# A recurrence moved two steps ahead on the grid of steps that a whole network shares, with the input products and base chunks dealt out anew

## What is computed

```
# block 0
att  = attention over 8 block sums, one vector per sequence, projected by Wo
n    = layernorm(x + att) * gamma + beta
q()  = block quantisation over groups of 32 values
x1   = x + q(silu(q(n) @ w_gate.T) * (q(n) @ w_up.T)) @ w_down.T      # inner width 2048

# block 1: a GRU over the 256 positions, state [16, 512], then a routed layer
gi   = x1 @ W_ih + b_ih
gh   = h @ W_hh + b_hh
r, z = sigmoid(gi_r + gh_r), sigmoid(gi_z + gh_z)
h    = (1 - z) * tanh(gi_n + r * gh_n) + z * h

hid    = silu(h @ rw1.T + rb1)
logits = hid @ rw2.T + rb2 + gates                # 16 experts, the top 2 are kept
coeff  = softmax of the top 2, zero elsewhere
y      = h @ W.T + bias + ((h @ A.T) * coeff) @ B.T
out    = x1 + y
```

## Time and profile before

| | |
|---|---|
| median of 3 runs | 1708.49 us (1707.1 to 1712.42) |
| the profiled execution: its own time | 1712.84 us |
| its span, first to last instruction | 1711.0 us |
| mean granted TensorE clock | 0.963 of full speed |
| busy: PE, PEld, DVE, ACT, POOL | 91%, 70%, 82%, 38%, 29% |
| granted TensorE clock in 40 slices, tenths of full speed | 9, 8, 6, 6, 6, then 9 in 34 slices and 8 in the last |

### The profile page before, as it was taken

The page is one execution under the profiler, slowest core; times in us unless marked ns, Lnnn a source line. Parts: engine busy times, 40 slices in busy tenths (PEclk is TensorE's granted clock), DMA queues, the critical chain, the costliest instruction groups (busy, mean ns, idle before and its releaser), DMA issues.

```text
span 1711.0 us, 75109 instructions
## 1 busy us (share of the span) xinstructions
PE 1551.7 (91%) x32268; PEld 1198.1 (70%) x32268; DVE 1399.7 (82%) x5571; ACT 644.3 (38%) x1624; POOL 496.8 (29%) x573
## 2 busy tenths in 40 slices
PE   5633689999999999999999999999999999999986
PEld 2321367777777777777777777777777777778874
DVE  7787888888888888888888888888888888887654
ACT  5666243333333333333333333333333333333331
POOL 6774322222222222222222222222222222221000
PEclk9866699999999999999999999999999999999998
DMA  7744211112211111122111112212111212211000
GB/s 245 267 154 135 57 45 43 42 47 49 49 46 49 31 40 49 46 46 50 48 41 49 49 46 49 37 35 47 46 46 49 49 43 46 49 43 37 25 15 20
DMA packets 122444, 101.01 MB, mean 59 GB/s; under 512 B 91904, under 2 KB 92288, under 8 KB 121728
## 3 DMA queue, kind: packets, MB, share of 16 engines
q1 hardware_dynamic: 121824, 96.02, 21.1%
q10 hardware_dynamic: 288, 0.19, 0.0%
HBM read 58.43 MB, written 16.78 MB: 44 GB/s over the span
## 4 chain that ended last, share of the span: by engine, by line
PE 77%; DVE 14%; issue 3%; DMA 2%; POOL 2%; ACT 2%; SPq 0%; DVEq 0%; ACTq 0%; POOLq 0%
PE ps_rn_turn L1311 25%; PE ps_gi L1212 12%; PE ps_z L1311 10%; PE ps_down L1179 6%; PE ps_gate_up L1170 6%; PE ps_gate_up L1160 4%; PE ps_base L1221 4%; PE ps_base L1264 3%; PE ps_route L1221 3%; DVE fe L821 1%; POOL qfT L1028 1%; DVE gi L630 1%; DVE gi L628 1%; DVE hT L808 1%; PE ps_rn_turn L1200 1%
## 5 line engine op out<-in xcount | busy, mean ns | idle before, releaser
L1311 PEld LDWEIGHTS ps_rn_turn<-hT,whh 128*128 128x128 f16 x16320 | 435.0, 96 | 86.0 <-DVE hT L759 72.2
L1311 PE MATMUL ps_rn_turn<-hT,whh 128*128 128x32 f16 x16320 | 449.3, 177 | 46.1 <-DVE hT L759 45.4
L1046 POOL TENSOR_TENSOR qf<-f8c,fe 128x512 bf16<-128x512 bf16 x128 | 134.1, 1047 | 862.1 <-DVE f8c L838 862.1
L583 ACT ACTIVATE r_tanh<-r_pre,scale_half 128x64 f32<-128x64 f32 x256 | 89.0, 348 | 563.5 <-DVE r_pre L779 563.5
L1212 PEld LDWEIGHTS ps_gi<-x1T,wih 128*128 128x128 f16 x4608 | 270.6, 98 | 32.8 <-issue 3.1
L1212 PE MATMUL ps_gi<-x1T,wih 128*128 128x128 f16 x4608 | 289.3, 220 | 1.6 <-ACT gi L574 1.6
L1311 PE MATMUL ps_z<-hT,whh 128*128 128x32 f16 x8160 | 243.3, 177 | 0.0
L1311 PEld LDWEIGHTS ps_z<-hT,whh 128*128 128x128 f16 x8160 | 222.6, 96 | 0.0
L574 ACT ACTIVATE gi<-ps_gi,b_i,scale_x 128x128 f32<-128x128 f32 x384 | 144.4, 456 | 196.7 <-PE ps_gi L1212 196.7
L773 DVE TENSOR_TENSOR r_half<-ps_rn_turn,gi 128x64 f32<-128x64 f32 x256 | 57.2, 224 | 149.9 <-PE ps_rn_turn L1311 146.1
L585 ACT ACTIVATE z_tanh<-z_pre,scale_half 128x64 f32<-128x64 f32 x256 | 89.0, 348 | 157.0 <-DVE z_pre L789 157.0
(11 more groups left out here) (201 smaller groups left out, 2408.5 us busy)
## 6 DMA issues: line engine op xcount, KB each, us to landing
wih<-in_x_steps SPq DMA_DIRECT2D x32, 256.0 KB, 5.4
xin<-in_x_steps SPq DMA_DIRECT2D x32, 256.0 KB, 2.9
xres<-in_x_steps SPq DMA_DIRECT2D x32, 256.0 KB, 3.0
x_dram<-x SPq DMA_DIRECT2D x32, 256.0 KB, 2.3
x_in_bias<-x_dram SPq DMA_DIRECT2D x32, 256.0 KB, 2.8
out_rows<-y SPq DMA_DIRECT2D x32, 256.0 KB, 2.0
stage<-in_ffn_w SPq DMA_DIRECT2D x12, 512.0 KB, 3.7
sg_gs<-in_ffn_w SPq DMA_DIRECT2D x12, 512.0 KB, 3.8
```

What stands on the lines that cost most here:

```text
L583: nc.scalar.activation(r_tanh[:, :], r_pre[:, :], ACT.Tanh, scale=HALF_S_INV).then_inc(r_ok, 1)
L1046: g.tensor_tensor(blocked(qf[:, :]), blocked(f8c[:, :]), spread(fe16[:, :]), ALU.mult).then_inc(qf_done, 1)
L1311: last = mm(ps[:, (at + j) * 2 * B:(at + j + 1) * 2 * B], whh[:, k, u, gate * D + j * P:gate * D + (j + 1) * P], hx(t)[:, 2 * k:2 * k + 2, ...
```

## The change

The recurrence, and with it routing and output, runs two steps ahead of where it was on the grid: in the slot (c, s) it handles the step number 8c + s + 2. The new function `recurrent(c, s)` gives its tile r and position b, and whether R (tile r) and L (tile r - 1) exist there. All of L's pieces are keyed by b instead of s, on all five engines, so route is in s = 6, hid_pre and hid in s = 7, turn_hid in s = 0 of the next c, and so on, and the experts' products and y in s = 5. Q, F, E and I stay where they are. W_ih's products, spread over s = 0 to 5 as 12, 36, 24, 24, 24, 24 matmuls, are spread over s = 0 to 4 as 24, 24, 48, 24, 24, and their evacuations move from s = 1, 3, 5 to 1, 2, 4. The four base chunks go to b = 0, 1, 2 and 6, that is s = 6, 7, 0 and 4. The waits between the users of ps_route are set anew for the new order, and FILL_UPS goes from 11 to 10. Nothing else moves, and no instruction of work is added or taken away.

```
-FILL_UPS = 11
+FILL_UPS = 10
+AHEAD = 2
-            return tuple(0 <= c + d < TILES for d in (4, 3, 2, 1, 0, -1))
+            return tuple(0 <= c + d < TILES for d in (4, 3, 2, 1))
+
+        def recurrent(c, s):
+
+            r, b = divmod(c * STEPS + s + AHEAD, STEPS)
+            return r, b, 0 <= r < TILES, 0 <= r - 1 < TILES
...
# SP
+                if L and b == 0:
+                    load_x1(r - 1)
+                if L and b == STEPS - 1:
+                    store_y(r - 1)
...
# ACT
-                if I and s in (1, 3, 5):
+                if I and s in (1, 2, 4):
...
# DVE: the same for every piece of L
-                if L and here == (6, 0):
+                if L and there == (6, 0):
...
# POOL
-                if L and s == 3:
+                if L and b == 3:
                     pool.wait_ge(x1in_loaded, count(l, 16, 16))
...
-                if L and s == 5:
+                if L and b == 5:
                     pool.wait_ge(gap_ok, count(l, 1, 1))
...
# PE
             def max_row(e, L):
 
                 pe.wait_ge(x_small, count(e, 6, 2))
+                wait(pe, x_scale_ok, count(e, 1))
                 if L:
-                    pe.wait_ge(l_small, count(e - 3, 6, 1))
+                    pe.wait_ge(wxaT_ok, count(e - 3, 1, 1))
...
                 if L:
-                    pe.wait_ge(wxaT_ok, count(e - 3, 1, 1))
+                    pe.wait_ge(xa_ok, count(e - 2, 1, 1))
                 mm(ps_x_scale, ones_b[:, :], x_row[:, :], start=True, stop=True).then_inc(x_scale_mm, 1)
...
                     wait(pe, wxaT_ok, count(l, 1))
-                    wait(pe, x_scale_ok, count(l + 2, 1, 1))
+                    wait(pe, x_small, count(l + 2, 6, 3))
...
                 pe.wait_ge(xa_ok, count(l, 1, 1))
+                pe.wait_ge(x_scale_ok, count(l + 2, 1, 1))
                 turn_(ps_h1T, hid[:, :], idf[:, :]).then_inc(hidT_mm, 1)
...
-            x_parts = ((0, (0,)), (0, (1, 2, 3)), (1, (0, 1)), (1, (2, 3)), (2, (0, 1)), (2, (2, 3)))
-            base_parts = {4: (0,), 6: (1, 2, 3)}
+            x_parts = ((0, (0, 1)), (0, (2, 3)), (1, (0, 1, 2, 3)), (2, (0, 1)), (2, (2, 3)))
+            base_parts = {0: (0,), 1: (1,), 2: (2,), 6: (3,)}
...
             def slot(c, s):
-                Q, F, E, I, R, L = stages(c)
+                Q, F, E, I = stages(c)
+                r, b, R, L = recurrent(c, s)
+                if (r, b) == (0, 0):
+                    pe.wait_ge(inter_done, FILL_UPS)
                 if R:
-                    pe.wait_ge(hx_ok, c * STEPS + (s + 1))
-                    t = c * STEPS + s - 1
+                    pe.wait_ge(hx_ok, r * STEPS + (b + 1))
+                    t = r * STEPS + b - 1
```

More of the change, by code:

```diff
@@ L360, in beside, with load_x1, store_y @@
                     slot(-4, p - FIRST_SLOT)
-            def loads(c):
-                Q, F, E, I, R, L = stages(c)
[L364 to L367, removed]
+            def load_x1(l):
+                wait(sp, x1b_done, count(l, 1))
+                sp.wait_ge(x1_stored, count(l, 1, 1) * 16)
+                sp.dma_start(x1_in[:, :], rows(x1_dram, l)).then_inc(x1in_loaded, 16)
+            def store_y(l):
+                sp.wait_ge(y_ok, count(l, 1, 1))
+                sp.dma_start(rows(out, l), y[:, :]).then_inc(y_stored, 16)
+            def loads(c):
+                Q, F, E, I = stages(c)
                 if E:
@@ L532, in weights, with others @@
                                          scale=S_L).then_inc(wl_hi, 1)
-            def others(c, s, Q, F, E, I, L):
-                f, e, i, l = c + 3, c + 2, c + 1, c - 1
-                if L and s == 1:
+            def others(c, s, Q, F, E, I, r, b, L):
+                f, e, i, l = c + 3, c + 2, c + 1, r - 1
+                if L and b == 1:
                     act.wait_ge(hp_ok, count(l, 1, 1))
                     nc.scalar.activation(hid[:, :], hid_pre[:, :], ACT.Silu).then_inc(hid_ok, 1)
-                if L and s == 5:
+                if L and b == 5:
                     act.wait_ge(l_small, count(l, 6, 6))
@@ L578, in slot @@
             def slot(c, s):
-                Q, F, E, I, R, L = stages(c)
+                Q, F, E, I = stages(c)
+                r, b, R, L = recurrent(c, s)
                 if R:
-                    t1 = c * STEPS + (s + 1)
+                    t1 = r * STEPS + (b + 1)
                     act.wait_ge(r_pre_ok, t1)
@@ L589, in slot @@
                     weights(c, s)
-                others(c, s, Q, F, E, I, L)
+                others(c, s, Q, F, E, I, r, b, L)
                 if c in (-3, -2):
@@ L862, in ffn, with others @@
                         clip(f8c, f8, f8_done, at, qf_done, f8c_done)
-            def others(c, s, place, Q, F, E, I, L):
-                q, e, i, l = c + 4, c + 2, c + 1, c - 1
+            def others(c, s, place, Q, F, E, I, r, b, L):
+                q, e, i, l = c + 4, c + 2, c + 1, r - 1
                 ffn(c, s, place, F, E)
-                here = (s, place)
-                if L and here == (1, 0):
+                here, there = (s, place), (b, place)
+                if L and there == (1, 0):
                     dve.wait_ge(xa_ok, count(l, 1, 1))
@@ L873, in others @@
                                            ALU.add).then_inc(hp_ok, 1)
-                if L and here == (4, 0):
+                if L and there == (4, 0):
                     dve.wait_ge(lg_mm, count(l, 1, 1))
                     v.tensor_tensor(lg0[:, :], ps_logit, rb2_b[:, :], ALU.add).then_inc(l_small, 1)
-                if L and here == (4, 1):
+                if L and there == (4, 1):
                     dve.wait_ge(l_small, count(l, 6, 1))
                     v.tensor_tensor(lg[:, :], lg0[:, :], gates_b[:, :], ALU.add).then_inc(l_small, 1)
-                if L and here == (4, 2):
+                if L and there == (4, 2):
                     dve.wait_ge(l_small, count(l, 6, 2))
                     v.max(top[:, :], lg[:, :]).then_inc(l_small, 1)
-                if L and here == (5, 1):
+                if L and there == (5, 1):
                     dve.wait_ge(l_small, count(l, 6, 3))
@@ L886, in others @@
                     v.tensor_tensor(gap[:, :], top[:, 0:1], top[:, 1:2], ALU.subtract).then_inc(l_small, 1)
-                if L and here == (5, 2):
+                if L and there == (5, 2):
                     dve.wait_ge(l_small, count(l, 6, 5))
                     v.tensor_copy(at_f[:, :], top_at[:, :]).then_inc(l_small, 1)
-                if L and here == (6, 0):
+                if L and there == (6, 0):
                     dve.wait_ge(coeff_ok, count(l, 3, 3))
@@ L946, in others @@
                     clip(q8c, q8, q8_done, count(q, 1), qx_done, q8c_done)
-                if L and here == (7, 3):
+                if L and there == (7, 3):
                     dve.wait_ge(y_mm, count(l, 1, 1))
@@ L958, in slot @@
             def slot(c, s):
-                Q, F, E, I, R, L = stages(c)
+                Q, F, E, I = stages(c)
+                r, b, R, L = recurrent(c, s)
                 def beside(place):
-                    others(c, s, place, Q, F, E, I, L)
+                    others(c, s, place, Q, F, E, I, r, b, L)
                 beside(0)
                 if R:
-                    recur(c, s, beside)
+                    recur(r, b, beside)
                 else:
@@ L1031, in slot @@
             def slot(c, s):
-                Q, F, E, I, R, L = stages(c)
-                q, f, e, l = c + 4, c + 3, c + 2, c - 1
+                Q, F, E, I = stages(c)
+                r, b, R, L = recurrent(c, s)
+                q, f, e, l = c + 4, c + 3, c + 2, r - 1
                 if Q and s == 0:
@@ L1283, in others @@
                     (gate, up)[s % 2](f, s // 2)
-                if L and s == 2:
+                if L and b == 2:
                     turn_hid(l)
-                if L and s == 3:
+                if L and b == 3:
                     logits(l)
-                if L and s == 6:
-                    turn_wxa(l, E)
-                if L and s == 0:
+                if L and b == 6:
+                    turn_wxa(l)
+                if L and b == 0:
                     route(l, range(KD))
@@ L1301, in others @@
                 if L:
-                    for k in (base_parts if R else base_parts_at_end).get(s, ()):
+                    for k in (base_parts if R else base_parts_at_end).get(b, ()):
                         base(l, k)
@@ L1344, in slot @@
                     pe.wait_ge(wih_lo, KD)
-                if (c, s) == (-1, 7):
-                    pe.wait_ge(inter_done, FILL_UPS)
-                if (c, s) == (1, 0):
+                if (r, b) == (1, 0):
                     pe.wait_ge(wl_lo, KD)
                     pe.wait_ge(bt_loaded, 16)
-                others(c, s, Q, F, E, I, R, L)
+                others(c, s, Q, F, E, I, r, b, R, L)
             pe.wait_ge(c_dve, 1)
```

19 lines of the change are left out of this document (7 added, 12 removed).

## The result

The changed kernel takes 1702.08 us (median of 6, 1700.75 to 1703.29), the kernel before 1709.65 us (median of 6, 1707.1 to 1712.42): ratio 0.9949, 95% interval 0.9935 to 0.9962. It is faster by 0.5%, 7.6 us by the medians, where 17.5 were forecast. 1702 lies inside the stated range (1677 to 1710), but above the stretch that the forecast itself named (1682 to 1699).

What follows compares the result with a forecast made beforehand. TensorE was taken to bound seven of eight steps, s2 ending in a 0.81 us wait. Full tiles -13.2 and ends -4.3 gave -17.5 us: 1695.3 for the profiled execution, 1691 against the median; range 1677 to 1710.

Steps and rivals of the forecast that it cites:

- TensorE's table: TensorE's work per step of a full tile, priced from the profile: sum 45.37 us against 46.47 before.
- s7: Eighth step of a tile, emptied to 4.97 us of TensorE work, meeting the floor of 4.91.
- s4: Fifth step, wxa ahead of x1 on VectorE: 5.66 us, 0.19 over TensorE's work.
- s1: Second step, now with GpSimd's x1 + bias: 5.90 us if rn gets through, 6.12 if rn is held.
- s2: Third step, 48 W_ih matmuls, VectorE held by GpSimd's multiply and add of beta: 6.38 us taken.
- one row of the fill: Add of beta in the fill took 1.80 instead of 1.27 us, read as VectorE's instructions going ahead of it.
- rival C: Slower: in s2 the add of beta precedes `finv`, delaying scales and z_half 1.27 us; s2 7.0; chance 0.11.
- rival B: Collisions eat the gain: rn held in s1, more in s2 or s4; 46.4 a tile, 1699 to 1708; chance 0.27.
- signs of being wrong: TensorE waiting in s5 or s6, wxa waiting for GpSimd's coeff, or the tile's period staying above 46.4.
- The ends: Fill and last tile together -3.9 us, c = 0 and c = 28 to 30 -0.4: in all -4.3 us.
- two steps in the fill: Recurrence's first two steps join c = -1, steps 6 and 7: about 5.0 + 5.0 us, so +6.0.
- The last tile: At c = 31 two recurrence steps of about 4.95 us fall away: -9.9 us.

Runs made afterwards that it cites:

- e4: Changed kernel with the two-step shift alone, W_ih products, evacuations and base chunks in their old portions: 1770.47 us, ratio 1.0351 to the kernel before.
- e5: Kernel before, without the shift, with only the new dealing of W_ih products, evacuations and base chunks: 1765.25 us, ratio 1.0314.
- e1: Changed kernel with GpSimd's x1 + bias moved from s1 to s0: 1682.69 us, ratio 0.9827 to the kernel before.
- e2: Changed kernel with VectorE's xn put ahead of inter and fam in s2: 1677.28 us, ratio 0.9798 to the kernel before.
- e6: Kernel before with VectorE's xn put ahead of inter and fam in s2, nothing else: 1692.97 us, ratio 0.9900.
- e3: Changed kernel with both x1 + bias moved to s0 and xn put first in s2: 1676.34 us, ratio 0.9788 to the kernel before.

## Why the prediction was wrong

**What bounds the kernel, and TensorE's table: right.** The prices read from one tile gave all steps in which TensorE decides, to 0.03 us, in the changed kernel and in e4 and e5 as well (5.36, 5.89, 5.48, 6.62, 5.55 here; 7.96 and 6.88 there). s7, the emptied step, was 5.01 against 4.97, and s4, where wxa goes ahead of x1, was 5.57 against 5.66.

**s1: the step right, the case wrong.** The forecast had rn get through and n_pre held. The addition started 0.14 us ahead of rn (1026.90 against 1027.04), and rn was held for 1.0 us. The starts had been put at 3.1 and 3.02 into s1 and were 2.85 and 2.99: VectorE came to s1 not 0.4 us later than before but 0.2 (rstd 2.31 into the step, before 2.12), and this was enough to turn the order round. For this case the text had 6.12 for s1. It cost less: with n_pre, the tanh and the rest close behind rn, the low part was just in time, and s1 stayed at 5.89.

**s2: the step that failed.** It stands in the sum with 6.38 and measured 6.82; 27 x 0.44 = 12 us, less 27 x 0.12 by which the other steps came out shorter. That leaves 27 x 0.32 = 8.6 us, and this is the whole miss in the full tiles. The prediction had the add of beta wait for VectorE's scales, by one row of the fill, and then hold rn. In the trace the add came in behind `finv` and held the third scale instruction (1.25 us), on which z_half and all behind it waited. In the fill it was one instruction, and a longer one, that had gone ahead of the add (210.38), by 0.02 us:

```profile
210.36 0.69 DVE L832 SCALAR_TENSOR_TENSOR f<-inter,finv 128x512 fp8e4<-128x512 f32 x1
```

In s2 `finv` had a like lead of 0.01 us, but it was over after 0.17, and what came next stood still. So the row of the fill did not say that all three scales go ahead. A block scale held by the add of beta, with z_half behind it, is the mechanism of rival C, one instruction later than described there, and it happened with s1 at 5.89: C's own sum for this case was 46.6 a tile and -1 us in all, the trace has 46.30. The result lies where rival B had put it (1699 to 1708), by C's mechanism. The order between the two engines hung on 0.01 us (1033.15 and 1033.16), as the text said that it would; to take a single value for it was the mistake. No run changes this order alone. What e1 and e2 show is that s2 falls to 6.09 and 5.95 once the add comes sooner, and 6.1 is what the text had for s2 without the collision in s1. None of the text's own signs of being wrong came true (46.30 is under its 46.4, TensorE does not wait in s5 or s6, wxa does not wait for the coefficients in a full tile): they were set too wide to catch this.

**What I did not see.** The wait in s2 of the kernel before was a hold of 0.70 us, the text said so, and then treated it as room to be filled. e6 shows that moving xn removes it for -17 us, and e2 and e3 show that the change then gets what TensorE's table promised: 45.43 a tile against its 45.37.

**The ends: -4.3 forecast, -5.0 measured** (-9.6 of span less 4.6 of tiles), by other parts, so that the agreement of the sum is in part luck. The two steps in the fill were priced 5.0 + 5.0 and took 5.05 + 5.24, but began at 221.12, not near 224; s0 of c = 0 begins 4.5 us later than before (231.41 and 226.87), not 6.0. The last tile gave -10.5 for -9.9, c = 0 and c = 28 to 30 together -0.6 for -0.4. The tail lost 1.5 us, nearly all to the clock, which no term held.

**Small terms.** The DMAs moved for nothing, as forecast: neither GpSimd nor VectorE waits for a DMA in a full tile. FILL_UPS was not tried by itself.

## What to carry to other kernels

Where two engines that exclude each other run interleaved, a table of work per step is only half a forecast: lay their starts and ends of the new order side by side, and where they fall within 0.1 us of each other price both orders and weight them, not one. Before filling a wait with work, ask which instruction ends it: if it is one that was held, move what holds it beside instructions that read PSUM. A piece that is moved carries its operands' conflicts into its new step, in both directions.

## What the runs showed of the hardware that I had not expected

VectorE's instructions of 16 columns were held twice in a row by two GpSimd instructions 0.08 us apart, the first for 0.67 us; one short instruction (`finv`) passed between them, and the next (0.17 us alone) was held for 1.08 us. gap, with a single column, was held for 0.82 us: the hold went by what was left of GpSimd's instruction, not by the size of VectorE's. GpSimd's fill of a 128x512 tile, which only writes, did not hold an instruction with two SBUF inputs that ran inside it (0.22 us).
